# A depthwise convolution with two group normalisations: the second channel's bands 0 and 1 of the last group finished in their transit buffers

## The reference, cut to what matters

```python
x = x + conv(gn(x), w)      # depthwise 6x11, input and output masked to the lower triangle
x = x + gn(x) + bias[h, i - j]   # bias table from a 3-layer network over the position i - j
```

## Time and profile before

| | us |
|---|---|
| median of 3 runs | 2648.5 (2640.96 to 2651.2) |
| the profiled execution, its own time | 2642.3 |
| its span, first to last instruction | 2640.6 |
| VectorE / TensorE / ScalarE / GpSimd busy in the span | 2296.1 / 1967.7 / 1659.4 / 1256.5 |
| moved by DMA | 901.17 MB, 341 GB/s over the span |

### The profile page before, as it was taken

The page is one execution under the profiler, slowest core; times in us unless marked ns, Lnnn a source line. Parts: engine busy times, 40 slices in busy tenths (PEclk is TensorE's granted clock), DMA queues, the critical chain, the costliest instruction groups (busy, mean ns, idle before and its releaser), DMA issues. The chain is left out here.

```text
span 2640.6 us, 76787 instructions
## 1 busy us (share of the span) xinstructions
PE 1967.7 (75%) x28880; PEld 1861.1 (70%) x28880; DVE 2296.1 (87%) x4175; ACT 1659.4 (63%) x3051; POOL 1256.5 (48%) x1988
## 2 busy tenths in 40 slices
PE   4289988877688886878788777888868787899700
PEld 0289887777687776877777776787768777888700
DVE  7799988899888997899898998989988899878745
ACT  2167766767567575666667566666657667687722
POOL 1123235535545454463555445554554546575543
PEclk9999999999889989989898999999989999999955
DMA  9775639999899999999999998999989998798899
GB/s 339 268 242 173 233 133 371 394 368 357 322 399 386 379 334 348 396 354 387 349 347 392 353 374 326 382 391 372 347 328 412 369 379 295 291 355 313 316 410 366
DMA packets 316250, 901.17 MB, mean 341 GB/s; under 512 B 42416, under 2 KB 42416, under 8 KB 314000
## 3 DMA queue, kind: packets, MB, share of 16 engines
q1 hardware_dynamic: 199648, 579.79, 59.5%
q10 hardware_dynamic: 116416, 319.37, 31.0%
HBM read 579.50 MB, written 319.68 MB: 341 GB/s over the span
## 5 line engine op out<-in xcount | busy, mean ns | idle before, releaser
L1162 PEld LDWEIGHTS psY<-wsplit,XT 128*128 128x128 f16 x25920 | 1590.0, 101 | 361.1 <-DVE XT L780 120.6
L1162 PE MATMUL psY<-wsplit,XT 128*128 128x168 f16 (+5 forms) x25920 | 1619.1, 222 | 293.6 <-DVE XT L780 241.0
L639 ACT CAST XT<-psT 128x512 f16<-128x512 f32 x720 | 415.1, 577 | 555.0 <-PE psT L1148 318.4
L1088 POOL COPY halo<-XT 128x16 f16<-128x16 f16 x720 | 314.7, 437 | 656.6 <-DVE XT L780 646.8
L780 DVE TENSOR_TENSOR XT<-psT,XT 128x512 f16<-128x512 f32 x720 | 493.4, 685 | 145.0 <-ACT XT L639 144.0
L1062 POOL TENSOR_TENSOR xn<-xn,mask 128x512 f32<-128x512 f32 x336 | 424.0, 1262 | 391.3 <-ACT xn L627 330.4
L808 DVE BATCH_NORM_STATS2 entries<-ring 128x6 f32<-128x512 f32 x872 | 551.3, 679 | 60.3 <-DMA ring<-in_x 59.9
L1148 PE MATMUL psT<-ident,xn 128*128 128x128 f32 x2880 | 480.4, 292 | 106.1 <-POOL xn L1062 87.5
L1097 POOL TENSOR_TENSOR ring<-ring,bias 128x1024 f32<-128x1024 f32 x184 | 416.4, 2265 | 270.4 <-ACT ring L687 270.2
L627 ACT ACTIVATE xn<-kept_c_band,normp 128x512 f32<-128x512 f32 (+2 forms) x496 | 398.4, 803 | 49.9 <-DMA kept_c_band<-in_x 31.9
L1148 PEld LDWEIGHTS psT<-ident,xn 128*128 128x128 f32 x2880 | 318.0, 146 | 116.1 <-POOL xn L1062 80.2
(11 more groups left out here) (78 smaller groups left out, 471.9 us busy)
## 6 DMA issues: line engine op xcount, KB each, us to landing
ring<-in_x SPq DMA_DIRECT2D x628, 512.0 KB, 8.7
out<-ring ACTq DMA_DIRECT2D x288, 512.0 KB, 6.5
kept_c_band<-in_x SPq DMA_DIRECT2D x224, 512.0 KB, 7.9
out<-kept_c_band ACTq DMA_DIRECT2D x224, 512.0 KB, 7.3
band<-in_x SPq DMA_DIRECT2D x48, 1024.0 KB, 11.3
out<-band ACTq DMA_DIRECT2D x48, 1024.0 KB, 8.8
ring<-out SPq DMA_DIRECT2D x96, 512.0 KB, 9.4
bias<-bias_scratch SPq DMA_DIRECT2D x16, 1793.5 KB, 8.7
```

Source lines behind the costliest of these rows:

```text
L639: nc.scalar.copy(XT[:, n % NB3, 0, :, 2:P + 2], psT[n % NB3][:, :, :]).then_inc(hi_ready, 1)
L1088: nc.gpsimd.tensor_copy(halo[:, t, :, :, :], XT[:, n % NB3, :, :, P:P + 2]).then_inc(halo_out, 1)
L1162: last = nc.tensor.matmul(psY[m][:, 0:rows, o + lo_c:o + hi_c], XT[:, m, xp, i, 2 - sh:2 - sh + P], wsplit[:, c, wp, K * sh:K * sh + rows, ...
```

## The change

Six units of the last group, those for which `stays` is true (18, 19 and 26 to 29: second channel, bands 0 and 1, lower blocks), are taken out of the list of loads. Their block stays in the transit buffer, where it was convolved, and the second layer is applied there and stored from there, under a semaphore of its own, `last_stored`. The three spills of the second channel in stage 8 (positions 51, 56 and 60) are left out. The engines and positions that finish the units are the same; the store of one that VectorE finishes stands two positions after it instead of one. Beside that, the bound of a load's position becomes -1 instead of 0: a load of the last group may stand at position 89 of stage 8, ahead of the bias table's load at that position.

Worked through by its own arithmetic, the planner gives these tables for group 7: units 0 to 3 are loaded at position 89 of stage 8 (before: position 0 of the tail); units 4 to 17 keep their places; units 20 and 21 are the only ones between unit 17 and the load of the second bias table (before: 18 to 21); behind that load stand 22 to 25 and 30 to 35 (before: 22 to 35). Units 32, 33, 34 and 35 take the buffers of 20, 21, 22 and 23 (before: of 24, 25, 26 and 27).

```diff
--- before.py
+++ after.py
@@ -239,15 +239,24 @@
 
 
     A_LEAD, U_LEAD, LAST_LEAD = 2, 3, 14
+
+    def stays(g, u):
+        c, b, q = STREAM[u][:3]
+        return g == G - 1 and c == CPG - 1 and q <= b
+
+    loads_at, uses_at, stores_at = {}, {}, {}
     planned = {}
     wanted = [(max(NT * g + at, NT - 1), "a", g, a) for g in range(1, G) for a, at in enumerate(STEADY.a)]
     for g in range(G):
         p = plan(g + 2 < G, g + 1 < G, True, on_dve)
         lead = U_LEAD if g + 1 < G else LAST_LEAD
         planned.update({(g, u): at for u, at in enumerate(p.u)})
-        wanted += [(NT * (g + 2) + max(at - lead, 0), "u", g, u) for u, at in enumerate(p.u)]
+        wanted += [(NT * (g + 2) + max(at - lead, -1), "u", g, u) for u, at in enumerate(p.u) if not stays(g, u)]
+        for u, at in enumerate(p.u):
+            if stays(g, u):
+                uses_at.setdefault(NT * (g + 2) + at, []).append(("u", g, u))
+                stores_at.setdefault(NT * (g + 2) + min(at + 2, NT - 1), []).append(("u", g, u))
     wanted.sort()
-    loads_at, uses_at, stores_at = {}, {}, {}
     buffer_of, load_count, store_count, held_by = {}, {}, {}, {}
     in_buffer = [("a", 0, max(range(i, NA0, NAB))) if i < NAB else None for i in range(NRING)]
     loads = [len(range(i, NA0, NAB)) if i < NAB else 0 for i in range(NRING)]
@@ -278,6 +287,10 @@
         uses_at.setdefault(use[kind], []).append(key)
         assert load < use[kind]
 
+    for table in (uses_at, stores_at):
+        for keys in table.values():
+            keys.sort()
+
     def units_at(table, kind, s, n):
 
         return [key for key in table.get(NT * s + n, []) if key[0] == kind]
@@ -382,6 +395,7 @@
         u_scaled = sem("u_scaled")
         u_added = sem("u_added")
         u_finished = sem("u_finished")
+        last_stored = sem("last_stored")
         u_stored = [sem(f"u_stored{i}") for i in range(NRING)]
         kept_done = sem("kept_done")
         bias_loaded = sem("bias_loaded")
@@ -438,6 +452,12 @@
         def unit_of(t, i, u):
 
             return t[:, i, :, :].rearrange("p h w -> p (h w)").rearrange("p (r w) -> p r w", r=u[5])
+
+        def stream_place(g, u):
+
+            if stays(g, u):
+                return part(transit[STREAM[u][1]], STREAM[u])
+            return unit_of(ring, buffer_of[("u", g, u)], STREAM[u])
 
 
         BIAS_KEPT = 1 - BW - VLO
@@ -681,9 +701,10 @@
 
             def scale_stream(g, u):
 
-                i = buffer_of[("u", g, u)]
-                v = ring[:, i, :, :]
-                act.wait_ge(ring_loaded[i], 16 * load_count[("u", g, u)])
+                if not stays(g, u):
+                    i = buffer_of[("u", g, u)]
+                    act.wait_ge(ring_loaded[i], 16 * load_count[("u", g, u)])
+                v = stream_place(g, u)
                 nc.scalar.activation(v, v, ACT.Identity, scale=col(outp, 0)
                                      ).then_inc(u_scaled, 1)
 
@@ -691,9 +712,8 @@
                 c, b = STREAM[u][:2]
                 of = u_before[on_dve[u]]
                 act.wait_ge(u_finished if on_dve[u] else u_added, of[NU] * g + of[u] + 1)
-                i = buffer_of[("u", g, u)]
-                act.dma_start(part(ov[chan(g, c), b], STREAM[u]), unit_of(ring, i, STREAM[u])
-                              ).then_inc(u_stored[i], 16)
+                stored = last_stored if stays(g, u) else u_stored[buffer_of[("u", g, u)]]
+                act.dma_start(part(ov[chan(g, c), b], STREAM[u]), stream_place(g, u)).then_inc(stored, 16)
 
             def stage(s, do_a, do_b, do_c, do_next):
                 ga, gb, gc = s, s - 1, s - 2
@@ -722,7 +742,7 @@
                             if PIECES[j][0] == n:
                                 piece(gb, j)
                         for i, at in spill_pos.items():
-                            if at == n:
+                            if at == n and not (gb == G - 1 and LOWER[i][0] == CPG - 1):
                                 spill(gb, i)
                     if do_a and n == ROOT1:
                         act.wait_ge(s1_root, s * 2 + 1)
@@ -752,7 +772,8 @@
             for i in range(NRING):
                 act.wait_ge(u_stored[i], 16 * stores[i])
             for s in x1_spilled.values():
-                act.wait_ge(s, 16 * CH)
+                act.wait_ge(s, 16 * (CH - 1))
+            act.wait_ge(last_stored, 16 * sum(stays(G - 1, u) for u in range(NU)))
 
 
         @block.vector
@@ -974,9 +995,10 @@
 
                 dve.wait_ge(bias_shifted, chan(g, STREAM[u][0]) + 1)
                 dve.wait_ge(bias_kept_shifted, g + 1)
-                i = buffer_of[("u", g, u)]
-                dve.wait_ge(ring_loaded[i], 16 * load_count[("u", g, u)])
-                v = unit_of(ring, i, STREAM[u])
+                if not stays(g, u):
+                    i = buffer_of[("u", g, u)]
+                    dve.wait_ge(ring_loaded[i], 16 * load_count[("u", g, u)])
+                v = stream_place(g, u)
                 nc.vector.scalar_tensor_tensor(out=v, in0=v, scalar=col(outp, 0), in1=bias_at(STREAM[u]),
                                                op0=ALU.mult, op1=ALU.add).then_inc(u_finished, 1)
 
@@ -1093,7 +1115,7 @@
                     wait_alone(pool, bias_shifted, chan(g, c) + 1)
                     wait_alone(pool, bias_kept_shifted, g + 1)
                 pool.wait_ge(u_scaled, N_POOL * g + u_before[0][u] + 1)
-                v = unit_of(ring, buffer_of[("u", g, u)], STREAM[u])
+                v = stream_place(g, u)
                 nc.gpsimd.tensor_tensor(v, v, bias_at(STREAM[u]), ALU.add).then_inc(u_added, 1)
 
             def stage(s, do_a, do_b, do_c, do_next):
```

## The result

| | before | after |
|---|---|---|
| median of 8 runs, us | 2642.92 (2638.98 to 2651.2) | 2633.47 (2628.07 to 2638.45) |
| profiled execution / its span, us | 2642.3 / 2640.6 | 2638.45 / 2636.7 |
| moved by DMA, MB | 901.17 | 894.88 |

The ratio is 0.9957 with a 95% interval of 0.9945 to 0.997: 11.4 us less, 8 to 14.5, and the two medians are 9.5 us apart. The forecast had 10.8 us, and put most of its chance on a change within 0.5%, where the ratio lies (its interval reaches to 0.55%). In absolute time it said 2638 and the median is 2633.47, inside the range of 2628 to 2646; it lies lower because the median of the kernel before, 2648.5 in the first three runs, is 2642.92 in eight. The profiled execution of after is 5 us slower than its median, so its stretches say more than its total. The moved bytes fell by 6.3 MB, the 3.15 MB written and 3.15 MB read that the diff promises.

What follows compares the result with a forecast made beforehand. TensorE and its feeders were taken to bound stage 8, and transfers most of the tail. Terms 0 + 1.8 + 3.0 + 6.0 = 10.8 us, from the median 2648.5 to 2637.7, rounded to 2638; range 2628 to 2646 us at 0.8.

Steps and rivals of the forecast that it cites:

- The spills left out: Stage 8, second channel: removing 3.15 MB of writes and three ScalarE issues gains 0; 1.8 us if ScalarE's queue were the bound.
- the cover: Stage 8: TensorE's work sets the pace and hides the spills, so leaving them out gains 0.
- a stage 8 that ends earlier: Sign that would show the whole prediction wrong, since it gave leaving out the spills nothing.
- The four loads ahead of the first bias table: Start of the tail: units 0 to 3 load earlier and shorten later queueing; 1.8 us, ends 0 and 5.2.
- The second bias table: Mid-tail: two loads fewer ahead of this table's load on SyncE's queue make it land sooner; 3.0 us.
- The second half: Tail after the second shift: four loads leave it, so the end comes sooner; 6.0 us, ends 4.9 and 7.8.
- the last scaling: End of the tail: ScalarE's scaling at 2626.65, released by a load, could start at 2625.0, 1.65 us sooner.
- the last four stores: End of the tail: they took 6.52 us, waiting for loads; without that they were given 1.6 us.
- every byte counts: Rival, chance 0.25: DMA alone sets the tail, so the gain is 16.5 us, to 2632.
- The compute chain holds: Rival, chance 0.22: DVE, ACT and POOL in order set both tail halves, second table no earlier; gain 4.9 us, 2643.6.
- The late first table: Rival, chance 0.05: the first bias table lands 22 us late behind the four loads; net 11 us slower, 2660.

## Why the prediction was right, and where it was not

The time and its sign came as forecast, and so did the kind of cause: a tail that was full of transfers, six loads taken out of it, and the compute chain next. The sum has four terms, and of these one was right and three were off: two too large in the profiles, one too small.

**The spills left out.** Taken as 0, with 1.8 us as the other end. The stretch of stage 8 shows 1.1. The bound held, and its reason (issues on ScalarE's queue) is where the trace of the tripled spills points. The step that failed is the cover, "TensorE sets the pace there": ScalarE's issues stand ahead of what feeds TensorE. The cover was read off the mean of the earlier trace rows, a DMA share of 0.86 over 122 us, but where the spills stand the share is 1.00. The prediction's own sign, a stage 8 that ends earlier, came true in small.

**The four loads ahead of the first bias table.** Taken as 1.8, half of the queueing seen in the chain. The three profiles of after have 62.68, 62.29 and 60.96 us for the stretch that it should shorten, before 62.05: 0. Alone it brought 0.3 us of tail, and 2.2 us of the medians, which the interval does not tell from 0. What failed, as the profiles have it, is the step from shorter queueing to a sooner end. With the early loads alone the store and load in the chain did get 2.3 us shorter, and the table and the rest gave nearly all of it back. In the kernel after they take 8.06 and 11.64, 8.01 and 11.28, and 6.92 and 10.55 us in the three profiles, against 7.24 and 10.46 without the early loads: nothing gained there. A full ring leaves the DMA engines with less to move early in the tail, as the windows show. That the four cost the bias table nothing was right: no wait for the first table arose.

**The second bias table.** Taken as 3.0; 8.21, 8.20 and 9.20 us against 11.53 are 3.0 in the mean. The size was right, and the kernel with two loads put back ahead showed that it is the place in the queue. The working, bytes at the queue's rate, was not: by it two more loads taken away would bring another 3 us, and they brought none. The rule by which the DMA engines take turns between queues (the Trainium skill, "DMA: Bandwidth & Descriptors", Queues, rings and completion order) would have given 5.2 us; the landing fell by 3.0.

**The second half.** Taken as 6.0, with 4.9 as its low end; 60.8, 60.3 and 61.0 against 64.1 are 3.4. The step that failed is the last scaling, which should start 1.65 us sooner, once its load is there. It starts 50.07 us after the second shift (2625.95), before 50.13 (2626.65). The last three scalings are 4.1 and 4.5 us apart instead of the 3.64 that I had read off one pair: the additions between them take 2.50 and 2.34 us (the chain above) where that pair had 2.0, and before the last one ScalarE issues the store of unit 31 too, which VectorE now finishes early. The other part, the last four stores, is as described but smaller: 2.96 instead of 6.52 us, where I had given them 1.6.

The terms come to 1.1 + 0 + 3.0 + 3.4 = 7.5 us in the profiles, where the prediction had 10.8 and the medians have 9.5, 11.5 and 10.9 in the three sets of runs. 7.5 lies just outside the interval of the result (8 to 14.5 us). The 2 to 4 us between are not located: the second channel of stage 8 begins at different times from run to run (2367.7 to 2374.4 us in all profiles but with no order by kernel), and the change issues nothing ahead of that point. The medians of the parts taken singly would fill the gap (3.2 us given back with the spills written once, 2.2 us for the early loads alone, against 1.1 and 0 in the profiles), but no interval separates either from its neighbour. This stays open. The total came nearer than its terms did: two were too large by 1.8 and 2.6 us, one too small by 1.1, and the 2 to 4 us that nobody located made up for it. As far as the runs show, that is luck.

Of the rivals, "every byte counts" is refuted by its 16.5 us, beyond the interval's 14.5, by the early loads alone and by the last 17 us at 265 GB/s. "The compute chain holds" described the second half better than the forecast did, and the wrong half of it was that the table would come no sooner. The late first table did not occur; its own price, 11 us slower, would have stayed within 0.5% too, so the 0.06 given to a slower kernel rested on no row. The reading of the Trainium skill's 358 GB/s ("DMA: Bandwidth & Descriptors", Where 436 GB/s comes from) made no difference: the tail of after moves 395 GB/s where it is full.

## What to carry to other kernels

Bytes taken out of a stretch that is full of transfers are worth what the next bound leaves of them: six loads of 7.8 us brought 3.4 us in the second half, because an engine's in-order list stood right behind. Look at that list before the sum is made, and try the instructions that wait for nobody ahead of the stores that do: it shortened the tail by 5 us in two profiles, and the medians by 0.9 us, which is not clear of noise. And a load issued shortly ahead of a long transfer that everything waits for costs its share of the queue, whatever the total of bytes; a prefetch into a ring that is full a moment later moves the pause and not the end.

## What the runs showed that I had not expected

The length of a DMA's issue is not a constant of the queue: on ScalarE's queue one of 0.52 MB took 0.34 us and up to 2.66 us when writes were tripled, and the compute instruction behind it and the three spills waited 5.37 us. 9.4 MB of writes that nobody waits for made the kernel 14 us slower (2645.79 against 2631.79 us), and it was not TensorE's clock: the mean granted clock is 0.920 in both profiles, and 1.00 in the window above where TensorE loses a fifth of its time. And the bias table of 1.84 MB, with nothing ahead of it, took 8.57 us, or 215 GB/s, while other transfers shared the DMA engines.
